# A decoder of twelve sections, two streams on one core: the order in which each engine takes its pieces, placed anew

## The reference

```python
x = x + L0_attn(_layernorm(x), ...)            # gated delta rule in chunks of 32, triangular inverses
x = x + L0_xattn(_layernorm(x), ctx, ctx, ...) # cross attention, 16 heads of 8
x = x + L0_ffn(_layernorm(x), ...)             # gated feed-forward part, 384 wide
x = x + L1_attn(...); x = x + L1_xattn(...)    # causal attention, then a mix with ctx
x = x + L1_ffn(_layernorm(x), ...)             # experts and a shared part
x = x + L2_attn(...); x = x + L2_xattn(...)    # causal attention, cross attention with a mask
x = x + L2_ffn(_layernorm(x), ...)             # 14 experts of 256, all of them computed
x = x + L3_attn(_layernorm(x), ...)            # state space scan, 16 states
x = x + L3_xattn(...)                          # cross attention, 4 query heads on 1
x = x + L3_ffn(_layernorm(x), ...)             # 8 experts of 512, capacity 512 tokens each
```

## Time and profile before

| | |
|---|---|
| median of 3 runs (lowest to highest) | 4756.86 us (4756.38 to 4769.69) |
| profiled execution: own time, span | 4767.48 us, 4765.8 us |
| the seven passes, in the span | 260.0 to 4165.9 us, 554.0 to 563.5 us each |
| ahead of them, the last stretch, experts and sums | 260.0, 446.8 and 153.1 us |
| TensorE, VectorE, ScalarE, GpSimd busy | 81%, 66%, 43%, 14% of the span |
| mean granted TensorE clock | 0.844 of full speed |

### The profile page before, as it was taken

How to read it: one execution, slowest core, us unless ns; L and a number is a source line. 1 busy time by engine, 2 the same in 40 slices (tenths; PEclk the granted TensorE clock), 3 DMA queues, 4 the chain that set the end, 5 groups by cost and what they waited for, 6 DMA issues and landing times. The chain is left out here.

```text
span 4765.8 us, 93107 instructions
## 1 busy us (share of the span) xinstructions
PE 3863.3 (81%) x36752; PEld 2707.5 (57%) x36752; DVE 3144.0 (66%) x8198; ACT 2051.9 (43%) x4873; POOL 678.6 (14%) x987
## 2 busy tenths in 40 slices
PE   1688888888878888788888888888888888889863
PEld 1456565655656565555656556565655656656642
DVE  3467767576765868677676767657686675765751
ACT  1236353454535454354534545353543535345520
POOL 1010201202020110202012020201102011120002
PEclk9679888798887988888888988879887897879886
DMA  4000000000000000000000000000000000000013
GB/s 130 1 2 1 7 2 7 2 1 7 1 7 1 6 2 1 8 1 7 2 7 2 1 7 1 7 1 6 2 1 8 1 6 2 6 2 1 1 35 91
DMA packets 69261, 45.67 MB, mean 10 GB/s; under 512 B 12995, under 2 KB 65852, under 8 KB 68590
## 3 DMA queue, kind: packets, MB, share of 16 engines
q1 hardware_dynamic: 63388, 33.03, 2.5%
q0 software_dynamic: 2048, 3.85, 0.3%
q10 hardware_dynamic: 3378, 2.64, 0.3%
HBM read 29.35 MB, written 10.50 MB: 8 GB/s over the span
## 5 line engine op out<-in xcount | busy, mean ns | idle before, releaser
L756 PE MATMUL banks<-scratch 32*128 32x512 f32 x2048 | 479.3, 741 | 45.3 <-DVE scratch L1741 17.6
L330 ACT ACT_TABLE_LOAD x321 | 411.8, 1283 | 13.3 <-PE banks L1083 7.8
L902 DVE TENSOR_REDUCE scratch<-banks 128x4 f32<-128x512 f32 x512 | 321.4, 681 | 76.8 <-PE banks L729 47.6
L1590 PE MATMUL banks<-scratch,w_ident 128*128 128x256 f32 x1024 | 298.8, 418 | 75.9 <-DVE scratch L1741 75.9
L1678 ACT ACTIVATE scratch<-scratch,ssm_A 128x256 f32<-128x256 f32 x512 | 231.4, 506 | 292.8 <-DVE scratch L1735 282.7
L866 ACT ACTIVATE scratch<-banks 128x512 f32<-128x512 f32 x512 | 269.9, 599 | 154.8 <-PE banks L790 154.1
L1874 PE MATMUL banks<-scratch 32*32 32x32 f32 x10496 | 274.0, 219 | 72.7 <-issue 44.8
L1735 DVE TENSOR_TENSOR_SCAN scratch<-scratch 128x512 f32<-128x512 f32 x256 | 312.9, 1222 | 15.4 <-ACT scratch L1678 8.6
L1874 PEld LDWEIGHTS banks<-scratch 32*32 32x32 f32 x10496 | 243.8, 131 | 123.4 <-issue 85.9
L581 POOL TENSOR_TENSOR 0_rstd<-0_var,minus_half 128x2 f32<-128x2 f32 x96 | 80.6, 840 | 1289.0 <-DVE 0_var L599 1079.3
L1590 PEld LDWEIGHTS banks<-scratch,w_ident 128*128 128x128 f32 x1024 | 191.9, 205 | 125.6 <-DVE scratch L1741 99.9
(11 more groups left out here) (516 smaller groups left out, 8635.3 us busy)
## 6 DMA issues: line engine op xcount, KB each, us to landing
experts<-in_e_W SPq DMA_DIRECT2D x16, 256.0 KB, 5.3
w_e_W<-in_e_W SPq DMA_DIRECT2D x3, 704.0 KB
expert_in<-scratch SPq DMA_DIRECT2D x1, 2048.0 KB, 14.1
scratch<-expert_in SPq DMA_DIRECT2D x8, 256.0 KB, 4.6
expert_out<-scratch SPq DMA_DIRECT2D x8, 256.0 KB, 2.3
scratch<-residual SPq DMA_DIRECT2D x8, 256.0 KB, 3.1
out<-scratch SPq DMA_DIRECT2D x8, 256.0 KB, 2.4
experts<-in_e_w SPq DMA_DIRECT2D x1, 1792.0 KB, 7.7
```

The lines of the kernel that those rows point to most:

```text
L330: act.preload_act_table_set(name)
L756: last = pe.matmul(row_tiles(t), lhs[r, col(s)], rhs[r, s], start=True, stop=letter == "S" and mask is None, skip_group_check=True)
L902: P.give(dve.tensor_reduce(negm[:, s, NI * j:NI * j + NI], row_tiles(t), X, ALU.max, negate=True), f"{nm}.S{s}{j}")
L1590: last = pe.matmul(total[:, c * N:(c + 1) * N], ident[:], yc[:, k % RING, j, :], start=False, stop=n == DS - 2 and j == 1, skip_group_chec ...
```

## The change

The sections, their pieces and the instructions in them stay as they are. The strings `TURNS` of TensorE, ScalarE, VectorE and GpSimd are written anew; SyncE's, and all of `LAST_TURNS` for the last stretch, stay. Compared piece by piece, 255 of TensorE's 660 pieces that hold instructions stand at another place in the pass, 122 of ScalarE's 426, 136 of VectorE's 522 and 9 of GpSimd's 68; most by one or two places, none by more than seven. TensorE's string has 113 "w" for 68 before. In the order of the pass the groups of "w" were 2, 7, 10, 7, 4, 3, 4, 10, 1, 1, 2, 14, 3 and are 2, 4, 7, 12, 10, 4, 12, 4, 4, 2, 1, 2, 7, 12, 6, 2, 8, 11, 3. ScalarE's table loads in a pass come to 37 by the new order, 41 before.

The core of the diff, with TensorE's strings whole, one line each of ScalarE's and GpSimd's as samples:

```diff
 TURNS = [
-    ("111ww0001000100110110001111000111wwwwwww11011111110000010000000011000100000001111111111110011011001011100100"
-     "001000110101111110111111111111111111111111111110111001110011110111111111001111001001111110100000011111111010"
-     "00111110000000110111wwwwwwwwww111001000111111110111101111wwwwwww11110000111111110011110111001001111111000000"
-     "0000000110111100wwww10100110001100000000000111001100100011101100110000110100000000011000000100000100000000ww"
-     "w0wwww000000110011100110000wwwwwwwwww0000100000000111w011110000011011100011111000000111000000111111111011101"
-     "001111100100011100000001110100000000110000000000000000000000000001000000000000011011100000001110000000100111"
-     "10000000001111100110000000110000111111101000000011w000111100000000010000000011ww0000110000000010101111101111"
-     "1001111001100000111000000000011010001111111110wwwwwwwwwwwwww1111111111www11111111111111111111111111111111111"
-     "11111111"),
...
-     "100101110000110001000000011111000110010111000010000110111011000011101000011111111111111111000001100000011101"
...
-    ("110010000000001110000001110000000110111100111111001111011100011111110000101110"),
+    ("111ww0001000010110110010111000111wwww110111111100wwwwwww1000000000011000100000100101111111110011100110111000"
+     "000011100011011111110011111111111111111111111111110111101011101011011111111110011101000111111100000011011111"
+     "100101101110000000110111wwwwwwwwwwww100111wwwwwwwwww10001101111111101wwww1111wwwwwwwwwwww1110010011111111001"
+     "01111110011110011011000001000000010111100wwww101000110010000100000001110011000001111011001100110001000000000"
+     "001100100000001000000000wwww0000011011100010100000000100000011100ww01110010001111101001101110000000011110000"
+     "11101100w011110011111110111100000000000111100000001100000000000000000000000000000000100001000001111000001100"
+     "100000001100110011000011000110ww0110011000011000011010000110wwwwwww0010wwwwwwwwwwww0001101110000wwwwww100001"
+     "00000000ww0000110100010000101011011111100111001111100011001000000000011wwwwwwww010001111111110wwwwwwwwwww111"
+     "1111111www1111111111111111111111111111111111111111111"),
...
+     "100011110000011001000011001110011000011011000010011000111011011100010000011111111111111100111100000000010111"
...
+    ("110001000000001110000001110000000101111101101111010111011100011111110000101110"),
     ("111000"),
 ]
```

More of the change, by code:

```diff
@@ L75 @@
-    ("111000110001000000101111100111100000000011000110000011111110011110000000000001101111111011111111101110111111"
-     "111001110110011101111111001000111111010001101111111110100110011100100010111001000111010000110000000001100100"
-     "100101110000110001000000011111000110010111000010000110111011000011101000011111111111111111000001100000011101"
-     "000000100000000010001000000001100000000111100000001100110000000100011100001010101111000110111010001101110111"
-     "11110011100000011001101111111111111111"),
@@ L80 @@
[L80 to L85, removed]
@@ new lines @@
+    ("111000111000000000101111100111100000000011100010001001111101110010100000000001101111111011111111101101111111"
+     "110101110011011110111111001000111111100001101111111101101100011001100100111000100110110010001000000001100010"
+     "100011110000011001000011001110011000011011000010011000111011011100010000011111111111111100111100000000010111"
+     "000000100000000000101000000000100000010111100000011001010000000100011100101000111011000110111100001101011111"
+     "11001110110000011001101111111111111111"),
@@ new lines @@
+    ("110010111111000000111111011110001000000011000000000000110110000001001000100111111110111111100000011110011100"
+     "010101101100100011000111001100010000000011111111001111100101011011111001110011101010111110101111110000010000"
+     "001111111100111001010101010011010111001101011011000111100010100100001000010000000100010000000000001100111001"
+     "110011101011101111101101111111000010000000111110011111100001110111011100010001011010110100100101001101110001"
+     "100000111111011111000000000110000000000011011001000011001010001001000010000010100011101111110110001100000011"
+     "000011001001001101011110111111111111111111111111"),
```

## The result

The changed kernel takes 4682.9 us, median of four runs (4669.9 to 4693.2), beside 4756.6 us of before (4749.4 to 4769.7). The ratio is 0.9859, with a 95% interval from 0.9836 to 0.9883: 1.4% or 74 us faster, where 48 us were forecast. The time lies inside the range.

What follows compares the result with a forecast made beforehand. No engine is full; TensorE, busy 81%, is the one to watch, its idle time winnable. Terms sum to -6.9 us a pass, x 7 = -48 us: 4709 us from 4756.9, range 4665 to 4785 (likeliest case 4670 to 4742).

Steps and rivals of the forecast that it cites:

- The two "w" terms: On TensorE: 64 added, one third uncovered, +2.3 us a pass; 19 removed, 3 of them not hidden by waits, -0.7.
- the clock term: Added matmuls keep TensorE active, so the mean clock rises from 0.851 to 0.86: -2.2 us a pass.
- Table loads: ScalarE, 37 loads for 41; gain mainly where delta-rule exps then run back to back: -0.6 us a pass.
- second delta rule: Second half of the delta rule beside the experts: output projection and norm transposes moved ahead of delta products, -3.0 us a pass.
- other waits: TensorE's other waits with re-ordered neighbours, 13.7 us in all; a fifth won, -2.7 us a pass.
- VectorE's three waits: Delta rule beside the experts: waits of 2.97, 3.68 and 2.73 us for TensorE, to fall below 9.4 together.
- rival 2: No change: order only moves waits, one stream gains what the other loses; 4743 to 4771 us, chance 0.15.
- the eight: TensorE waits of 0.98 to 2.81 us with re-ordered neighbours, 13.7 us in all, six for a hn.
- The slower rival: Mamba rounds: added "w" uncovered, delaying scans; hT copy or table load ahead of decays; 4780 us, chance 0.21.
- The much faster rival: Clock at 0.88, 4672 us, or re-ordered waits give 6 to 8 us more, 4660 to 4670; chance 0.14.

Runs made afterwards that it cites:

- the second stretch: Only 140 to 280 us of the pass in the new order, with 18 "w" more, against the kernel before: 4790.7 us, ratio 1.0085.
- the first: Only the first 140 us of the pass in the new order, with its "w", against the kernel before: 4724.6 us, ratio 0.9939.
- the last: Only 400 us to the end of the pass in the new order, with 31 "w" more, against the kernel before: 4713.4 us, ratio 0.9913.
- the old order: The kernel before with its order kept, but TensorE has the 113 "w" of the changed kernel: 4745.2 us, ratio 0.9981.
- the columns of the table: Old and new order, each with no, 68 or 113 "w" in a pass, against the kernel before; with none, 4780.3 and 4709.5 us.
- the third stretch: Only 280 to 400 us of the pass in the new order, with 8 "w" fewer, against the kernel before: 4727.8 us, ratio 0.9943.
- The first delta rule: Only 52 to 92 us of the pass in the new order, no "w" touched, against the kernel before: 4730.9 us, ratio 0.9951.

## Why the prediction was right, and where its sizes were off

**Direction and mechanism held.** The order fills waits, the "w" cost about as much as they give, and the barrier makes each pass show it. The sum was too small by a third: -6.9 us a pass where the two traces show -10.7. That the total lies in the range is in part luck: the second stretch loses 5.8 us a pass (0.0085 of 4754), which no term holds, and the first and the last win 4.3 and 5.9 us, which the terms didn't place there.

**The two "w" terms and the clock term.** They were +2.3 for uncovered "w", -0.7 for those removed and -2.2 for the clock, -0.6 together. Measured: 0.9981 in the old order, 9 us or 1.3 us a pass (from 2.9 faster to 0.2 slower, by the interval). In the new order 0.0005, 0.3 us a pass. So their sum was right within what can be measured; the three were not measured one by one, and an error in one can hide behind another. The Trainium skill, "TensorE: Matmul & The Clock Gate", section "What's actually happening", says that activity releases the throttle; the columns of the table agree, 0.833 to 0.844 and 0.834 to 0.857 for 68 "w". What I had wrong is who brings the clock of the changed kernel: with the old "w" and the new order it is 0.857 already (0.855 over all executions, of 0.859). The price per 0.01, 2.5 us, was rather small; two passes of one kernel give 3.5.

**The order terms were mis-sized.** Table loads, second delta rule and other waits were -0.6 - 3.0 - 2.7 = -6.3 us a pass; the order with the old "w" is worth 0.0136 x 4752.0 / 7 = 9.2 us (5.8 to 12.6). The forecast is at the low edge of that interval; without any "w" the order is worth 10.0 us (7 to 13), and there it lies outside. By parts:

- The second delta rule, with the table loads, gives 27 us or 3.8 us a pass, for 3.6 forecast. The number is right, but the way there isn't the one that I named. I expected VectorE's three waits to shrink below 9.4 us together. The timeline of VectorE in the changed kernel, at the place of the earlier trace rows:

```profile
2257.56 0.29 DVE L2160 TENSOR_TENSOR scratch<-scratch,banks 128x128 f32<-128x128 f32 x1 [3.04 <-PE banks L1874]
...
2260.47 0.42 DVE L610 TENSOR_TENSOR 0_xres<-0_xres,banks 128x256 f32<-128x256 f32 x1 [0.58 <-PE banks L826]
...
2272.12 0.29 DVE L2168 TENSOR_TENSOR scratch<-scratch,banks 64x128 f32<-64x128 f32 x1 [8.75 <-PE banks L1874]
```

The wait for the output projection fell from 3.68 to 0.58 us, but the wait for the last delta products rose from 2.73 to 8.75, so the three are 12.4 us. VectorE idles more at this place and the pass is shorter, since the residual sum L610, from which stream 0's next norm follows, comes 2260.47 - 1904.7 = 355.8 us after the barrier, and not 360.8. It was a trade between two chains, as rival 2 said, only not an even one.
- The exps came together as read, with one load ahead of the four:

```profile
2204.98 1.28 ACT L330 ACT_TABLE_LOAD   x1
2206.27 2.06 ACT L866 ACTIVATE scratch<-banks 128x512 f32<-128x512 f32 x4
```

The 37 loads came true (293 in the kernel): two of the four fall away in the third stretch and two in the last (307 in either of these runs). No run priced them by themselves.
- The first delta rule is where the term for the other waits fell short. I gave it a share of -2.7 and singled out a turn there that lets a delta sum wait; by itself that stretch is worth 23 us, 3.3 us a pass. The views that I read to price it were the named waits. The idle time that the new order removed is the 1.47 us that the profile calls "issue", which I had left out of the eight: a wait for a delta sum that stood behind L893 on VectorE, in the very place where I saw only a sum made to wait.
- The last stretch gives 41 us, 5.9 a pass; in its own trace 4.1 us of this lie between the first scan and the last, the largest step (2.7 us) at the fourth. There I had seen only "w" that might overrun.

**The slower rival was half right.** It named the mamba rounds, decays behind a table load or an hT copy, and uncovered "w". In stream 1's mamba this is measured: 1.0085 for the stretch, half of it from the order, and a kernel that leaves it out takes 4665.5 us. But it is one stretch of two; the rounds of stream 0, with 31 more "w", gain.

**The much faster rival** asked for 0.88 of clock or 6 to 8 us more from the waits. The clock didn't come; of the waits came some 3 us a pass.

## What to carry to other kernels

Where two streams share in-order engines, price a new interleaving by stretches: cut both orders where they have issued the same pieces, run each stretch alone, and keep those that win; here three of four did. Look at idle time that the profile calls "issue" as well as at named waits: it can be a wait for another engine, which is found by asking what that engine did before it took the step that was needed. Judge a trade between two chains by when the longer one's next norm begins, not by an engine's idle time. Fillers for the clock and the order of real work are two things: time the order without any filler first.

## What the runs showed of the hardware that I had not expected

Passes of one kernel, with the same instructions in the same order, differ by 2 to 3% (546.9 to 562.9 us in the run with the third stretch alone), and with them the clock. Of the fastest kernel, the windows of its shortest and its longest pass:

```profile
1887.20:2426.00 538.80, 462.09 (x4573) 325.93 (x4573) 386.65 (x1018) 245.98 (x601) 80.68 (x118) 0.88 0.01 4
2426.00:2976.60 550.60, 474.01 (x4573) 333.30 (x4573) 387.07 (x1018) 247.19 (x601) 80.30 (x118) 0.85 0.01 4
```

11.8 us for 0.03 of clock as rounded here, 0.022 by the trace's clock records (0.877 and 0.854). So a stretch that is not changed can gain or lose some us behind one that is: in the run with the third stretch alone, stream 0 was 3.5 us late at 264 us of the pass, ahead of all that the edit touches. A difference of a few us at one place of one trace is no price; the whole kernel's ratio is.
